# Gate projection ahead of the transposition of y in slots 0 and 1, and k of chunks 0 and 1 transposed into other PSUM banks

## What is computed

```python
xn = layernorm(x)
# attention, 8 heads of 64
q = phi(xn @ W_Q.T); k = phi(xn @ W_K.T); v = xn @ W_V.T      # phi = elu + 1
S = gamma * S + k_t v_t^T ; z = gamma * z + k_t               # over the tokens
y = (S^T q_t) / (z . q_t + 1e-6) * sigmoid(xn @ W_g_w.T + W_g_b)
attn = y @ W_O.T
# feed-forward: linear plus two of eight rank-4 experts, softmax weights
ffn = xn @ W_lin.T + b_lin + sum_k w_k * (xn @ left[idx_k]) @ right[idx_k]
out = x + attn + ffn
```

## Time and profile before

| what | value |
|---|---|
| time, median of 3 runs | 261.59 us (261.1 to 263.84) |
| time of the profiled execution | 263.04 us |
| its span on the slowest core (core 5) | 262.0 us |
| spans of all eight cores | 258.1 to 262.0 us |
| busy share of PE / DVE / ACT / POOL | 91% / 62% / 29% / 24% |
| S_blk on POOL (L323), mean of its 30 instructions | 0.969 us |
| granted TensorE clock, mean of a core | 0.998 to 1.000, 9 tenths or more in each of the 40 slices |

### The profile page before, as it was taken

The page is one execution under the profiler, slowest core; times in us unless marked ns, Lnnn a source line. Parts: engine busy times, 40 slices in busy tenths (PEclk is TensorE's granted clock), DMA queues, the critical chain, the costliest instruction groups (busy, mean ns, idle before and its releaser), DMA issues.

```text
span 262.0 us, 5276 instructions; the slowest of 8 cores (258.1 to 262.0 us)
## 1 busy us (share of the span) xinstructions
PE 238.8 (91%) x1688; PEld 117.4 (45%) x1688; DVE 162.4 (62%) x425; ACT 76.0 (29%) x128; POOL 61.7 (24%) x99
## 2 busy tenths in 40 slices
PE   0348999999897999999999999999999999999995
PEld 0223454454453555444454555444545454445442
DVE  5365457658857657666566657557566776687522
ACT  2563765576163323312322021111111201000000
POOL 2761100011134230505050402112214030333000
PEclk9999999999999999999999999999999999999999
DMA  6999999999986226352327232233222224343423
GB/s 174 207 175 255 251 169 206 233 181 180 245 219 102 83 60 184 101 155 67 118 78 129 83 101 83 88 94 103 81 100 83 101 83 124 136 140 108 159 104 136
DMA packets 20366, 35.86 MB, mean 137 GB/s; under 512 B 12210, under 2 KB 12530, under 8 KB 20084
## 3 DMA queue, kind: packets, MB, share of 16 engines
q1 hardware_dynamic: 17444, 24.89, 32.9%
q0 software_dynamic: 2896, 10.64, 21.5%
HBM read 32.00 MB, written 8.39 MB: 154 GB/s over the span
## 4 chain that ended last, share of the span: by engine, by line
PE 84%; DVE 6%; DMA 4%; issue 3%; ACT 1%; SPq 0%; DVEq 0%; ACTq 0%
PE PJ L365 26%; PE L L387 17%; PE L L431 9%; PE PJ L358 7%; PE PJ L387 4%; PE L L365 4%; DMA x_sb<-x 4%; PE PJ L431 2%; PE L L358 2%; PE T L336 2%; PE SY L379 2%; PE SY L403 2%; PE T L344 1%; PE T L417 1%; PE SY L407 1%
## 5 line engine op out<-in xcount | busy, mean ns | idle before, releaser
L387 PE MATMUL L<-wlin_sb,xnfm 128*128 128x512 bf16 x208 | 49.2, 379 | 0.0
L323 POOL TENSOR_SCALAR S_blk<-S_sb,small_s 128x260 bf16<-128x260 f32 x30 | 28.6, 969 | 82.7 <-DVE S_sb L814 82.5
L387 PEld LDWEIGHTS L<-wlin_sb,xnfm 128*128 128x128 bf16 x208 | 20.0, 98 | 24.1 <-issue 0.8
L885 ACT ACTIVATE e_sb<-PJ 128x512 bf16<-128x512 f32 x28 | 16.5, 594 | 41.2 <-PE PJ L365 39.7
L643 DVE TENSOR_SCALAR e_sb<-e_sb 128x512 bf16<-128x512 bf16 x32 | 9.7, 303 | 30.0 <-ACT e_sb L885 30.0
L861 ACT ACTIVATE xn_tm<-x_sb,nmr,rstd 128x1024 bf16<-128x1024 f32 x16 | 19.9, 1245 | 25.4 <-POOL nmr L279 23.8
L431 PE MATMUL L<-wo_sb,ygfm 128*128 128x512 bf16 x104 | 26.7, 379 | 0.0
L365 PE MATMUL PJ<-xnfm,wq_sb 128*128 128x512 bf16 x112 | 26.6, 380 | 0.0
L365 PE MATMUL PJ<-xnfm,wg_sb 128*128 128x512 bf16 x112 | 26.6, 379 | 0.0
L365 PE MATMUL PJ<-xnfm,wk_sb 128*128 128x512 bf16 x112 | 26.6, 380 | 0.0
L358 PE MATMUL PJ<-wv_sb,xnfm 128*128 128x512 bf16 x96 | 24.6, 400 | 0.0
(11 more groups left out here) (116 smaller groups left out, 339.0 us busy)
## 6 DMA issues: line engine op xcount, KB each, us to landing
ro_sb<-x SPq DMA_DIRECT2D x16, 512.0 KB, 4.0
out<-ro_sb SPq DMA_DIRECT2D x15, 512.0 KB, 2.7
x_sb<-x SPq DMA_DIRECT2D x10, 512.0 KB, 9.1
x_sb<-x POOLq DMA_DIRECT2D x6, 512.0 KB, 20.5
wlin_sb<-wlin POOLq DMA_DIRECT2D x1, 2048.0 KB, 38.0
wv_sb<-wv POOLq DMA_DIRECT2D x4, 256.0 KB, 11.8
wq_sb<-wq POOLq DMA_DIRECT2D x2, 512.0 KB, 17.6
wk_sb<-wk POOLq DMA_DIRECT2D x2, 512.0 KB, 24.4
```

The lines of the kernel that those rows point to most:

```text
L323: GP.tensor_scalar(S_blk[:, :].rearrange("p (q w) -> p q w", q=4)[:, :, 65 * e : 65 * e + 65], S_sb[:, :].rearrange("p (q w) -> p q w", q= ...
L387: TE.matmul(lb(c, n)[:, :], xnk(k, c), wlin_sb[:, D * k + 512 * n : D * k + 512 * n + 512], start=False, stop=False)
L885: SE.activation(e_sb[:, 512 * (n % 2) : 512 * (n % 2) + 512], bank[:, :], AF.Exp).then_inc(ac_e, 1)
```

## The change

Two edits. First, in slots 0 and 1 the gate projection (8 matmuls of 512 columns into PJ1) is issued right after `vslot`, ahead of `ytr` (and of `tht` in slot 0); from slot 2 on its place is as before. Second, `ktr(0)` and `ktr(1)` write into L0 and L1 in place of T1, and DVE's `ktm_sb` reads them there. With that `ktr(1)` no longer waits for the gate multiplication of slot 0 (`dv_gate` 1) but for ACT's `vev(7)`; the wait for `dv_gate` 1 stands before `state(1)`. `ktr(2)` and `ktr(3)` stay in T1 and wait for `dv_gate` 2 and 3 as before. No instruction but waits is added or removed.

```diff
+    KT = [L[0][:, 0:256].bitcast(BF16), L[1][:, 0:256].bitcast(BF16),
+          T1[:, 0:512], T1[:, 0:512]]
     ring4 = [PJ[0], PJ[1], L[0], L[1]]
@@ ktr
-            ins = TE.transpose(T1[:, 128 * p : 128 * p + 128], fmc(kfm, c)[:, p, :],
+            ins = TE.transpose(KT[c][:, 128 * p : 128 * p + 128], fmc(kfm, c)[:, p, :],
                                ident[:, :])
+    def gproj(c):
+        TE.wait_ge(dv_k, c + 5)
+        fproj(wg_sb, c // 4 + 1, c % 4, PJ[1], pe_g)
@@ pe_program, slot c
             TE.wait_ge(dv_k, 4 * b + 4)
-            if c == 0:
-                TE.wait_ge(dv_xev, 8)
+            if c < LAG:
+                TE.wait_ge(ac_v, 7 + c)
             elif c < 4:
                 TE.wait_ge(dv_gate, c)
             if c < 4:
@@
             av(c)
             if c < NCH - 1:
                 TE.wait_ge(dv_ktm, c + 1)
-                if c >= 4:
+                if c == 0:
+                    TE.wait_ge(dv_xev, 8)
+                elif c < LAG or c >= 4:
                     TE.wait_ge(dv_gate, c)
                 state(c)
@@
                 o_group(lo, 0)
                 lin_group(lo, 1)
-            elif c + 8 < NCH:
+            else:
                 vslot(c)
+                gproj(c)
             TE.wait_ge(dv_norm, c + 1)
@@
             if lo >= 0:
                 o_group(lo, 1)
-            if more:
-                TE.wait_ge(dv_k, c + 5)
-                fproj(wg_sb, b + 1, s, PJ[1], pe_g)
+            if lo >= 0 and more:
+                gproj(c)
@@ dve_program, slot c
             if c < 4:
                 VE.wait_ge(pe_ktr, c + 1)
-                ktile = T1[:, 0:512]
+                ktile = KT[c]
```

## The result

The changed kernel took 263.74 us (median of 20 runs, 263.13 to 264.74), the kernel before 262.00 us (median of 20 runs in the same sessions). The ratio is 1.0068 with a 95% interval of 1.0052 to 1.0083: slower by 0.7%, or 1.7 us, where 261.6 us and a range of 260.3 to 263.0 had been forecast. That is less than 1%, but it is clear of noise and outside the range. Executions in which a whole die ran at a granted clock of 0.83 to 0.85 (one of the kernel with ACT first, one of slot 1 only, 1.3 us later) are left out of all counts and ratios.

A forecast was written before the change was run, and what follows sets the result against it. PE's instruction stream was taken to bound the kernel, so only pauses could shrink: slot 0 -1.24, slot 1 up to `kproj(1)` +1.10 and +0.14, after it 0, total 0.0 us, giving 261.6 us, range 260.3 to 263.0.

The forecast's parts named there:

- What bounds the kernel, the four pauses: PE's instruction stream bounds; its pauses before `ytr(0)`, `ktr(1)`, `ytr(1)`, `ktr(2)` (0.77, 0.47, 1.40, 0.82) total 3.46 us.
- Part 1, slot 0: Slot 0 on PE: the pauses before `ytr(0)` and `ktr(1)` vanish, putting PE 1.24 us ahead at `ktr(1)`.
- the lead: PE's gain in slot 0, at `ktr(1)`: 1.24 us, the first two pauses, 0.77 + 0.47.
- Part 2, the lead is lost on ACT: Slot 1 up to `kproj(1)`: ACT's copy and tanh bind; 1.10 us pause before `xtr(9)`, 0.14 before `kproj(1)`.
- Part 3, slot 1: Slot 1 after `kproj(1)`: `ytr(1)` without pause, `ktr(2)` at its old time behind one 2.22 us pause; sum 0.
- The unpriced: Terms taken as 0 but bounded: ACT-to-PE release at 0 gives 261.45, DVE and POOL excluding each other 261.9; bank reads no difference.
- POOL was not held up: Rival at POOL's bias of chunk 10: held up by DVE's `ktm_sb`, up to 0.33 us late, 261.9 us; chance 0.07.
- the term of the clock: TensorE's clock falling in the pause before `ktr(2)`: taken as 0, by the size the skill page names.
- the sum: Slot 0 -1.24, slot 1 to `kproj(1)` +1.10 and +0.14, after it -1.40 - 0.82 + 2.22; total 0.0 us.
- a rival with a chance of 0.04: PE's clock falls in the 2.22 us pause before `ktr(2)`: 3.4 us more, 265.0 us, 1.3% slower; chance 0.04.
- The rule weighed there: Skill page on idle stretches sending the array to half rate; read as making the 2.22 us pause still short enough, term 0.
- the clock case: The rival that PE's clock falls after the pause before `ktr(2)`: 265.0 us, chance 0.04, left out of the range.

The follow-up runs named there:

- the kernel with ACT first: The changed kernel with ACT's copy and tanh of the gate ahead of the norming of chunk c+10 in slots 0 and 1; 261.19 us, ratio 0.9949.
- slot 1 only, 1.3 us later: The kernel before with the gate projection early in slot 1 alone, plus 6 idle matmuls ahead of slot 1's k projection; ratio 1.0069.
- both edits: The changed kernel with k of chunk 2 transposed into T0, and ACT's copy and tanh ahead of the norming in slots 0 and 1; 258.58 us, ratio 0.9863.
- runs with 1.63 us: The changed kernel with 2 idle matmuls of 512 columns ahead of the transposition of k of chunk 2; ratio 1.0029.

## Why the prediction was wrong

**What bounds the kernel, the four pauses**: right. Filling them all gave 3.6 us (both edits) against 3.46 counted.

**Part 1, slot 0**: right. `ytr(0)`, `tht(0)` and `ktr(1)` follow without idle, and the gate multiplication starts 2.47 us after S on DVE as before (69.84 - 67.37 and 71.01 - 68.54). The two groups of transpositions took 69.24 - 68.80 = 0.44 us, not 0.52, so the lead at `ktr(1)` was 1.33 us, not 1.24.

**Part 2, the lead is lost on ACT**: right. The pause ahead of chunk 9 is 1.20 us by the idle column, and by starts, as the forecast counts, 72.99 - 69.89 - 1.74 = 1.36 against 1.10. It is released by ACT's copy, with 0.25 us from its end to PE's start, not 0.15; the k projection starts 0.15 after the tanh. Measured from v's projection it starts at 8.15 us, against 8.07 before: the lead is lost completely. The prediction's sentence that the seven other cores of before show the same fit holds for five of them; on cores 0 and 6 the k projection started 0.38 us after the tanh, so these had 0.2 us to spare. Putting ACT's two instructions ahead gave the lead back.

**Part 3, slot 1**: right. 16.59 us from v's projection to `ktr(2)` against 16.5 forecast, one pause of 2.22 us by starts.

**The unpriced**: POOL was not held up (0.26 us under DVE's read of k), the banks cost nothing (ratio 1.0001). The place that was drawn on from the Trainium skill (SBUF — State Buffer, "Who interferes with whom") agrees with that row.

**The step that failed is the term of the clock**: the sum puts slot 1 after the k projection at -1.40 - 0.82 + 2.22 = 0, as if a pause cost its own length and nothing more, and leaves the fall of the clock to a rival with a chance of 0.04 and the wrong size. The runs showed +1.6 us in its place. The mechanism stood in the rival with its place. It was weighed with the sentence that 2.22 us is nearer to the harmless 1.24 than to 4.30, a reading between two far ends where nothing had been measured. The measured curve at this place is steep: harmless at 1.20 us, 1 core in 9 at 1.63, 3 in 4 at 1.84, 9 in 10 at 2.06. With eight cores and the slowest one counting, even 1 core in 9 shows in most runs (7 of 10 runs with 1.63 us). The price was taken from the slow stretch of the prologue, 16 matmuls, 3.4 us; measured were 1.6 to 1.7 us: PE, at work without pauses, had its clock back after about 8 matmuls. And the slow stretch of the prologue was no fall behind the 4.30 us at all. PE ran at the slow pace from its first instructions on, before that pause (kernel before, core 5):

```profile
8.95 1.01 PE L336 MATMUL T<-ident_s,xn_tm 128*128 128x128 bf16 x8 [8.95 <-ACT xn_tm L861]
11.29 1.01 PE L336 MATMUL T<-ident_s,xn_tm 128*128 128x128 bf16 x8 [1.33 <-ACT xn_tm L861]
```

Eight such transpositions take 0.61 us once the clock is up. The granted clock that "reads full there" is only the lack of a record: the record begins at 26.04 us. So the rows had no fall behind any pause, neither the length that brings it on nor its price, and "nearer to 1.24 than to 4.30" compared 2.22 us with a pause that had shown nothing. The time of the rival, 265.0, was too high and the forecast 261.6 too low; the truth lay between.

The rule weighed there, of the Trainium skill (TensorE: Matmul & The Clock Gate, "HAM oscillation — how this bites in real kernels"), named a larger idle gap than this one as what throttles the array again. The trace disagrees: 2.06 us did it on 148 of 160 cores, and the measurement decides.

**The range** ended at 263.0 because the clock case, with its chance of 0.04, was left out. The cost of that case, sized at 1.3%, and the lack of any row between 1.24 and 4.30 us should have given it a chance that the range could not leave out.

## What to carry to other kernels

An edit that only moves a wait is not neutral: two pauses of 1.2 and 0.7 us with dense work between them (by the idle column) and the same two in one piece of 2.06 us hold PE up equally long, 2.22 us by starts, but the one piece cost another 1.7 us through TensorE's clock. When waits are regrouped, look at the longest pause that results and at where it lies, and count the cores whose clock falls, not the median core; idle matmuls in the pause are a quick test and cost nothing when PE would wait anyway. Follow a lead to the next engine whose program order holds it (here ACT, and T1's last reader on DVE), and free that first: the reordering then paid 1.4% in place of losing 0.7%.

## What the runs showed of the hardware

- A pause of 2.06 us on PE, in one piece, with 0.9 us of small matmuls behind it, was followed by a granted clock of 0.5 for the next 3.4 us on 148 of 160 cores. The clock came back while PE was busy with 8 matmuls of 512 columns at the 1.2 GHz level; cost 1.6 to 1.7 us.
- The same pause 1.3 us later in the program was followed by a fall on 7 of 48 cores. The length of a pause alone does not tell whether the clock falls; how long after the core's own rise of the clock it began parted the 30 profiled cores that fell from the 9 that did not, without an exception.
- 8 matmuls of 512 columns for nothing made a kernel 1.5 to 1.9 us faster (262.28 us beside a kernel before of 262.27, against 263.74 beside 262.00).
- PE ran at the slow pace from its first instruction up to 26.04 us (kernel before, core 5), while the view gave a granted clock of 1.00: ahead of a core's first clock record that number says nothing.
